# Channel-wise denominators in a linear attention, and four pieces of its surroundings in another order

## The reference

```python
x = x + hyena_conv(layernorm(x))        # short conv, long conv by DFT, gating
x = x + ffn(layernorm(x))               # first mixture of experts
x = x + linear_attention(layernorm(x))
x = x + ffn(layernorm(x))               # second mixture, the same weights
```

```python
q, k = elu(q) + 1, elu(k) + 1
S = S + k[..., :, None] * v[..., None, :]      # running state
z = z + k                                      # running sum of keys
num = einsum('bhi,bhij->bhj', q, S)
den = sum(q * z, axis=-1, keepdims=True)       # one number per token and head
y = num / (den + 1e-6);  return y @ w_proj
```

## Time and profile before

| | us |
|---|---|
| median of 3 runs | 563.15 |
| lowest and highest | 560.63, 567.77 |
| the profiled execution | 564.55 |
| its span from first to last instruction | 562.7 |

### The profile page before, as it was taken

The page is one execution under the profiler, slowest core; times in us unless marked ns, Lnnn a source line. Parts: engine busy times, 40 slices in busy tenths (PEclk is TensorE's granted clock), DMA queues, the critical chain, the costliest instruction groups (busy, mean ns, idle before and its releaser), DMA issues.

```text
span 562.7 us, 13019 instructions
## 1 busy us (share of the span) xinstructions
PE 485.5 (86%) x3852; PEld 372.8 (66%) x3852; DVE 360.7 (64%) x1134; ACT 267.0 (47%) x715; POOL 329.0 (58%) x448
## 2 busy tenths in 40 slices
PE   3989999987888888887899999998878869888883
PEld 1668778865656888864566666666655546888861
DVE  6598999667556455445777787678665545545534
ACT  3554444524532444434777668666543513434430
POOL 4454776277460555552998888888476440555540
PEclk9999999989789999999999999999888889999997
DMA  8999900001011222215000000000011111222228
GB/s 285 320 403 405 404 34 0 2 23 48 29 49 33 77 78 77 77 38 151 1 2 2 2 3 2 3 1 2 3 42 48 33 46 30 77 69 77 71 76 257
DMA packets 36993, 47.56 MB, mean 85 GB/s; under 512 B 4186, under 2 KB 28123, under 8 KB 36798
## 3 DMA queue, kind: packets, MB, share of 16 engines
q1 hardware_dynamic: 31648, 35.90, 19.6%
q0 software_dynamic: 4544, 9.35, 4.9%
q10 hardware_dynamic: 734, 1.50, 0.8%
HBM read 17.86 MB, written 28.87 MB: 83 GB/s over the span
## 4 chain that ended last, share of the span: by engine, by line
PE 66%; DVE 9%; ACT 9%; issue 8%; another core or an unknown queue 4%; POOL 1%; DVEq 1%; DMA 0%; ACTq 0%; POOLq 0%
PE bank L778 61%; ACT silu_sh L1232 2%; PE bank L305 2%; DVE prod L1593 1%; ACT row_in_t L1207 1%; PE bank L888 1%; ACT wide L1207 1%; ACT rows L1225 1%; DVE conv_xv L1500 1%; ACT scores_odd L1207 1%; PE bank L1168 1%; PE bank L790 1%; ACT k_tok L1207 1%; DVE residual L1599 1%
## 5 line engine op out<-in xcount | busy, mean ns | idle before, releaser
L658 POOL DMA_INDIRECT routed<-row_out,row_token x78 | 75.1, 963 | 93.8 <-ACT row_out L1207 61.1
L778 PE MATMUL bank<-row_in_t,row_weights 128*128 128x128 f32 x624 | 84.9, 279 | 15.8 <-ACT row_in_t L1207 12.4
L778 PEld LDWEIGHTS bank<-row_in_t,row_weights 128*128 128x128 f32 x624 | 75.7, 191 | 21.8 <-ACT row_in_t L1207 15.6
L649 POOL DMA_INDIRECT sorted_rows<-rows,place x64 | 62.8, 981 | 38.2 <-issue 15.3
L1273 ACT ACTIVATE row_silu<-bank 128x256 f32<-128x256 f32 x78 | 30.2, 387 | 68.7 <-PE bank L778 48.1
L1645 DVE TENSOR_TENSOR row_act<-row_silu,bank 128x256 f32<-128x256 f32 x78 | 32.7, 419 | 40.1 <-ACT row_silu L1273 24.9
L778 PE MATMUL bank<-wide,weights_sb 128*128 128x512 f32 x112 | 56.1, 642 | 0.0
L778 PE MATMUL bank<-weights_sb,prod 128*128 128x128 f32 x256 | 39.7, 306 | 16.1 <-DVE residual L1599 8.2
L1232 ACT ACTIVATE silu_sh<-bank 128x512 f32<-128x512 f32 x32 | 18.9, 595 | 72.6 <-PE bank L778 54.5
L778 PEld LDWEIGHTS bank<-weights_sb,prod 128*128 128x128 f32 x256 | 34.8, 212 | 24.4 <-DVE residual L1599 11.7
L778 PE MATMUL bank<-experts,row_act 128*128 x312 | 49.5, 281 | 1.1 <-ACT row_out L1207 0.6
(11 more groups left out here) (192 smaller groups left out, 1092.8 us busy)
## 6 DMA issues: line engine op xcount, KB each, us to landing
sorted_rows<-zeros SPq DMA_DIRECT2D x1, 17028.0 KB, 50.9
row_in<-sorted_rows SPq DMA_DIRECT2D x78, 64.5 KB
rows<-routed SPq DMA_DIRECT2D x8, 256.0 KB, 4.9
scores_odd<-routed SPq DMA_DIRECT2D x8, 256.0 KB, 4.4
out<-residual SPq DMA_DIRECT2D x8, 256.0 KB, 3.0
routed<-row_out,row_token POOLq DMA_INDIRECT x78
tables_sb<-tables SPq DMA_DIRECT2D x1, 1024.0 KB, 9.0
experts<-rt_gate SPq DMA_DIRECT2D x1, 1024.0 KB, 18.2
```

Of the source, the lines that this page charges most:

```text
L649: pool.indirect_dma_start(sorted_rows, bass.IndirectOffsetOnAxis(ap=place[:, t:t + 1].bitcast(U32), axis=0), rows[:, t, :], None).then_inc ...
L658: pool.indirect_dma_start(routed, bass.IndirectOffsetOnAxis(ap=row_token[:, r:r + 1].bitcast(U32), axis=0), row_out[:, r, :], None).then_i ...
L778: return pe.matmul(out_, lhsT, rhs, start=start, stop=stop, **kw)
```

## The change

Six things change. **One**, the denominators are made in channel layout at once: PE multiplies by `own_head` (128x128, ones where two channels have the same head), which sums over a head and spreads in one matmul of 256 columns into bank 0; ACT adds epsilon while copying it to SBUF (`att_den_copy`); DVE inverts 128x256 numbers in place. The spreading copy, the two transposes and the old copy are gone. **Two**, in DVE's iteration `att_shift` of batch n+5 stands ahead of this inversion, instead of in the next iteration. **Three**, POOL's `pair_rstd` of the second mixture are spread over iterations 3 to 12, rank and place of pair 0 move one iteration forward, and with them its sends, from iteration 14 to 13. **Four**, at the attention's opening the first mixture's last `down` and its `gate_up` move behind the first batches' norm, and DVE makes two of the four masked copies of q of batch 0. **Five**, ACT issues an Exp of one element ahead of the attention. **Six**, at the kernel's end the additions of pairs 2 to 6 stand ahead of `add_shared` of the last pair.

```diff
-        den_wide, recip = spect_y[:, 0, 0:L], spect_y[:, 0, L:2 * L]
-        den = sb("den", [P, AT * HEADS])
+        den = spect_y[:, :, 0:L]
...
             pipelined([(2, att_qz), (3, att_by_head), (2, clear_future(0)), (5, att_rstd), (2, clear_future(1)),
-                       (0, beside({10: rstds(0), 11: rstds(1), 12: rstds(2, 3), 13: rstds(4, 5), 14: first_send,
-                                   15: second_send}, 2))], B, 2)
+                       (0, beside({3: rstds(0), 5: rstds(1), 7: rstds(2), 9: rstds(3), 10: rstds(4), 12: rstds(5),
+                                   13: first_send, 14: second_send}, 2))], B, 2)
...
                 pe.wait_ge(a_qz, b + 1)
-                wait(pe, a_y, b)
-                for t in range(AT):
-                    last = mm(pe, bank[2][:, 2 * P + t * HEADS:2 * P + (t + 1) * HEADS], qz[:, r, t * P:(t + 1) * P],
-                              head_of)
-                last.then_inc(a_den_mm, 1)
+                pe.wait_ge(a_v, min(b + 2, B))
+                wait(pe, a_den_copied, b)
+                if b == B - 1:
+                    pe.wait_ge(e_route, routed_to("is_top", 1, 0))
+                mm(pe, bank[0][:, L:2 * L], own_head, qz[:, r, :]).then_inc(a_den_mm, 1)
...
-            pipelined([(2, att_scores(0)), (0, att_out), (1, att_recip), (4, att_turn), (1, att_values), (2, att_scores(1)),
-                       (2, att_turn_keys), (0, beside({12: gates_at(0), 13: gates_at(1), 14: opening, 15: closing}, 2)),
-                       (4, att_project), (2, att_state), (2, att_den),
-                       (0, beside({11: turns(0), 12: turns(1), 13: turns(2)}, 2))], B, 2)
+            pipelined([(2, att_scores(0)), (0, att_out), (4, att_turn), (2, att_den), (1, att_values), (2, att_scores(1)),
+                       (2, att_turn_keys), (0, beside({12: gates_at(0), 13: second_gate, 14: opening, 15: closing}, 2)),
+                       (4, att_project), (2, att_state),
+                       (0, beside({11: turns(0), 12: turns(1), 13: turns(2)}, 2))], B, 2, beside_batches)
...
+            act.activation(held[:, 14:15], held[:, 15:16], ACT.Exp)
...
+                act.activation(den[:, r, :], bank[0][:, L:2 * L], ACT.Identity, bias=held[:, 12:13]
+                               ).then_inc(a_den_copied, 1)
...
-                gate_up(LATER + 1, 0)
...
+            def att_first_by_head(i, r):
+                if (i, r) == (0, 0):
+                    dve.wait_ge(a_qk, 1)
+                    for j in FIRST_BY_VECTOR:
+                        dve.tensor_scalar(q_by_head[:, 0, j, :], qk(0)[:, 0:L], head_in_group[:, j:j + 1], 1.0,
+                                          ALU.mult, ALU.mult).then_inc(a_first_by_head, 1)
...
-                dve.tensor_scalar(den[:], bank[2][:, 2 * P:2 * P + AT * HEADS], ATT_EPS, None, ALU.add
-                                  ).then_inc(a_den, 1)
-                dve.wait_ge(a_den, 2 * b + 1)
-                dve.reciprocal(den[:], den[:]).then_inc(a_den, 1)
+                dve.wait_ge(a_den_copied, b + 1)
+                dve.reciprocal(den[:, r, :], den[:, r, :]).then_inc(a_den, 1)
...
-            pipelined([(1, att_den), (1, att_state), (4, att_shift), (3, att_feature_sum), (2, att_mask(0)), (0, att_add),
+            pipelined([(1, att_state), (3, att_feature_sum), (3, att_first_by_head), (2, att_mask(0)), (0, att_add),
                        (5, att_in), (0, att_stats), (3, att_k_sum), (0, beside({14: third_apply}, 2)), (1, att_divide),
-                       (2, att_mask(1)), (0, beside({11: first_apply, 12: first_choice, 13: second_choice,
+                       (2, att_mask(1)), (5, att_shift), (2, att_den), (0, beside({11: first_apply, 12: first_choice, 13: second_choice,
                                                      14: third_choice, 15: third_place}, 2))],
-                      B, 2, {-4: later_gate_up, -3: later_add})
+                      B, 2, {-4: later_gate_up, -3: second_gate_up, -2: later_add})
...
             add_routed(dve, 1, 0, PAIR)
+            gate_up(LATER + 1, 0)
+            add_routed(dve, 1, PAIR, PAIR)
             gate_up(LATER + 1, 1)
-            add_routed(dve, 1, PAIR, PAIR)
+            for k in range(2, LATER + 1):
+                add_routed(dve, 1, k * PAIR, PAIR)
             add_shared(LATER + 1)
-            for k in range(2, PAIRS):
-                add_routed(dve, 1, k * PAIR, PAIR)
+            add_routed(dve, 1, (LATER + 1) * PAIR, PAIR)
```

More of the change, by code:

```diff
@@ L49 @@
 WE = 2 * I + IB * D
-CONSTS = 8
+CONSTS = 9
 RT = TILES + E - 1
@@ L671, in _ @@
             pool.memset(held[:, 13:14], 0.5).then_inc(const_made, 1)
+            pool.memset(held[:, 12:13], ATT_EPS).then_inc(const_made, 1)
             pool.wait_ge(const_made, CONSTS - 2)
@@ L736, in att_by_head @@
                 wait(pool, a_score, AT * GROUPS * (b - 1))
-                for j in range(IN_GROUP):
+                if b == 1:
+                    pool.wait_ge(e_down, PAIRS)
+                heads = range(IN_GROUP) if b else FIRST_BY_POOL
+                for j in heads:
                     pool.tensor_scalar(q_by_head[:, r, j, :], qk(b)[:, 0:L], head_in_group[:, j:j + 1], 1.0,
-                                       ALU.mult, ALU.mult).then_inc(a_by_head, 1)
+                                       ALU.mult, ALU.mult).then_inc(a_by_head, IN_GROUP // len(heads))
             def clear_future(t):
@@ L810, in rank @@
                 pe.wait_ge(e_route, routed_to("chosen_b", m, k))
+                if k == 0 and m == 1:
+                    pe.wait_ge(a_masked, N_MASKED * B)
                 if K:
@@ L922, in row_tiles, with last_down @@
                 up(LATER + 1)
+            def last_down():
                 down(LATER + 1)
-            return turn, gate, rank, up_half, pairs, row_tiles
+            return turn, gate, rank, up_half, pairs, row_tiles, last_down
         @block.tensor
@@ L1032, in tables_there @@
                 pe.wait_ge(tables_loaded, 16)
-            turn, gate, rank, up_half, pairs, row_tiles = experts_pe(pe, 0)
+            turn, gate, rank, up_half, pairs, row_tiles, last_down = experts_pe(pe, 0)
             def first_turn():
@@ L1158, in att_values @@
                 last.then_inc(a_values, 1)
-            def att_recip(i, r):
-                b = 2 * i + r
-                pe.wait_ge(a_wide, b + 1)
-                pe.wait_ge(a_v, min(b + 3, B))
-                if b >= B - 2:
-                    pe.wait_ge(e_route, routed_to("is_top", 1, b - (B - 2)))
-                for t in range(AT):
-                    last = pe.transpose(bank[0][:, (2 + t) * P:(3 + t) * P], den_wide[:, t * P:(t + 1) * P], ident)
-                last.then_inc(a_recip, 1)
             def att_out(i, r):
@@ L1177, in att_out @@
                 last.then_inc(a_out, 1)
-            turn, gate, rank, up_half, pairs, row_tiles = experts_pe(pe, 1)
+            beside_batches = {-3: last_down}
+            turn, gate, rank, up_half, pairs, row_tiles, last_down = experts_pe(pe, 1)
             def turns(k):
@@ L1922, in second_choice @@
             def second_choice():
+                find_place(0)
                 choose(1)
@@ L1929, in third_choice @@
             def third_choice():
-                find_place(0)
+                find_place(1)
                 gate_up(0, 0)
                 choose(2)
-                find_place(1)
             def third_place():
```

52 lines of the change are left out of this document (27 added, 25 removed).

## The result

| | before | changed |
|---|---|---|
| median, us (20 runs each) | 563.49 | 566.87 |
| lowest, highest | 559.0, 568.14 | 560.17, 571.81 |
| the profiled execution's span | 562.7 | 563.3 |

The ratio of changed to before is 1.009, 95% interval 1.0058 to 1.0122: slower by about 5 us, where 1.4 us less was forecast (a median of 561.7, within 553 to 570). On another chip the changed kernel gave 1.0057 [1.0021, 1.0093], with medians of 566.86 and 564.44.

The account below looks back on a forecast made before the run. PE was taken to set the attention's pace, with POOL 1 us and DVE 2 us behind. -4.7 + 0.8 + 3.3 + 0 + 0.2 - 1.0 = -1.4 us against the median 563.15 gave 561.7 us, range 553 to 570.

Parts of the forecast that it names:

- Step 3: Second-mixture rstds in iterations 3, 5, 7, 9: POOL overflows, delay mostly covered; 0.2 each, +0.8 us, bounds 0 and 2.9.
- the two loops: In the attention, dependencies through mask, shift, inversion and state, or feature sum and POOL's rstd: both stay under 7.83 us.
- step 2: DVE's inversion in the attention loop takes 1.76 us and stays covered; gain 0.39 us for each of 12 batches, -4.7.
- Steps 1 and 2: Attention loop: PE's dropped transposes cut the period from 8.22 to 7.83 us; the inversion at 1.76 us stays covered; -4.7.
- Step 4: Attention's end, iterations 11 to 13: the longer inversion delays normalisations PE waits for; +0.9, +0.4 and +2.0, in all +3.3 us.
- step 5: Scatter one iteration earlier: first scatter some 7 us earlier, but no effect on PE's row tiles; 0 us.
- Step 6: Attention's opening: moved table load, Exp and copies gain nothing; the moved down stands ahead of batch 1's turn; +0.2 us.
- Step 7: Kernel's end: one addition instead of six behind add_shared, output DMAs already full; -1.0 us, between 0 and 3.1 gained.
- Rival A: Attention's middle: the inversion becomes the bound on DVE, from 2.09 us upward; 566.8 us, or 575.9 at 2.82; chance 0.25.

Follow-up runs that it names:

- edge: Changed kernel with second-mixture rstds 0 to 2 in iterations 11 to 13 behind q times key sum, 3 to 5 ahead of the first scatters: 0.9966, repeated 0.9973.
- Experiments 2 to 4: Early rstds alone on the kernel before: 1.0024; changed kernel, early rstds behind q times key sum: 1.0053; changed kernel, denominator matmul behind values: 1.0068, without early rstds 1.0051.
- experiment 10: Earlier scatter undone or isolated in several kernels; the one cited here, rank, place and scatters of pairs 0 and 1 an iteration earlier on the kernel before: 1.0005.
- experiment 5: Changed kernel with the inversion on 32 of the 256 columns, the other 224 left uninverted: 1.0050.
- experiment 11: Changed kernel with the opening as before: 1.0087; the changed kernel once more: 1.0057.
- the kernel of experiment 9: Kernel before with only the denominators in channel layout and the shift ahead of the inversion (parts one and two): 1.0024.
- the first one of experiment 10: Changed kernel with all of part three undone: rstds late, rank, place and scatters of pairs 0 and 1 an iteration later: 1.0031.
- experiment 3: Changed kernel with each early rstd of the second mixture issued by POOL behind q times key sum instead of ahead of it: 1.0053.
- experiment 8: As edge, with DVE's normalisations of pairs 0, 1 and 2 in iterations 11 to 13 ahead of the inversion: 1.0021 against the kernel before.

## Why the prediction was wrong

**Step 3 failed.** "I take 0.2 each, +0.8 us", with the words that most of it is covered because the matmul starts 2 us after the scores. Each of the four costs 1.0, 4.0 us in all, above even the bound of 2.9. A fifth stands ahead of `value_c` in iteration 10, in both kernels (rstd 0 before, rstd 4 now). Step 3 did not count it; with the matmul at the iteration's end it was free. Now it costs 1.0 too: the period from batch 13 to 14 is 11.19, and 10.18 in edge, which has no rstd there. In both PE waits 1.53 us for the turn of that period:

```profile
388.39 0.66 PE L793 MATMUL bank<-tables_sb,normed 128*128 128x128 f32 x4 [1.53 <-DVE normed L1502]
```

That makes 5.0 us. Undoing the early rstds takes the ratio from 1.009 and 1.0057 to 0.9986 and 0.9984, 4 to 6 us, across chips.

The bound was wrong because I priced POOL's overflow of work (0.73) and not the arrival of `value_c`. By arrival it is 0.23 + 1.85 + 0.72 = 2.80 us behind the scores, for a matmul that could start at 1.94. The rows of before would have given about half of that: with this trace's 0.23, 0.23 + 1.33 + 0.88 = 2.44. The rest is that the rstd took 1.85 us here. Experiments 2 to 4 show the mechanism: alone it is free, behind `value_c` it costs 0.58, and with the matmul moved 0.38. In these two the delay goes from POOL's own rstd to shift, inversion and `state`, parts of the two loops that step 2 named and held to stay under the period.

**Steps 1 and 2.** The transposes are gone and the inversion is right within 0.02 us. The period is 7.98, not 7.83. Before, PE's starts were 0.33 us apart from the state matmul (of keys and values) to what follows, and 0.55 from the output projection to what follows (300.67 in the earlier trace rows):

```profile
298.28 0.49 PE L778 MATMUL bank<-v_wide,k_tok 128*128 128x128 f32 x2 [0.29 <-ACT k_tok L1207]
298.61 0.52 PE L778 MATMUL bank<-tables_sb,value_c 128*128 128x16 f32 x4
...
300.12 0.71 PE L778 MATMUL bank<-weights_sb,gated 128*128 128x128 f32 x4
```

In the changed kernel they are 0.41 to the scores and 0.62 to the turn:

```profile
301.30 0.49 PE L781 MATMUL bank<-v_wide,k_tok 128*128 128x128 f32 x2 [0.29 <-ACT k_tok L1214]
301.71 1.14 PE L781 MATMUL bank<-prod,silu_sh 32*128 32x512 f32 x8
302.79 0.71 PE L781 MATMUL bank<-weights_sb,gated 128*128 128x128 f32 x4
303.41 0.41 PE L305 MATMUL bank<-tables_sb,normed 128*128 128x128 f32 x2
```

That is -0.24 and not -0.39 a batch: -2.9 for -4.7. The estimate of 2.22 us from the Trainium skill ("VectorE: DVE Perf Modes", section "First, the fixed hardware budget"), its repeat count of 8 read as cycles a column, does not hold here: from 32 to 256 columns the inversion grows from 0.353 to 1.744 us, 6.2 ns each.

**Step 4.** Predicted +3.3. From the first scores of batch 13 to the last values the changed kernel needs 4.5 us more (2.1, 1.3 and 1.1), of which 1.0 is the rstd's of iteration 10. PE waits 1.53, 1.09 and 3.17 us ahead of the three turns, where it waited 0.23, nothing and 1.44. The earlier scatter, which step 5 put at nothing, can arise in the same stretch; on the kernel before it adds 4.0 up to the last values (experiment 10). The inversion's own share is smaller than I thought: taken away almost whole (experiment 5), it takes 1.8 off the three waits and 0.7 off the last values. The size was near, the reason half right.

**Step 5** said 0 and the time says 0 on the kernel before, by two effects of 4 us that cancel, which I had not seen. **Step 6** said +0.2; it is +2.5 and +1.3 on the spot in the two profiles. The step that it left out is PE's clock behind the idle 3.06 us. The idle time itself costs nothing, as the first turn starts 6.66 us after the last `up` began and did so at 6.62 before; and where the clock stayed at 1.00 the first scores came at 13.4. At the end no gain from undoing it is seen (experiment 11). **Step 7** said -1.0. The output queue is as full (share 1.12 at 557 to 560, 1.01 before) and the last addition is 0.6 later in the profile, 0.1 counted from the last `up`. Steps 6 and 7 together are worth nothing that can be told: the kernel of experiment 9 has neither, the first one of experiment 10 has both, and they gave 1.0024 and 1.0031 on one chip.

With the rstds at 5.0 instead of 0.8, the loop at -2.9 instead of -4.7, and the rest as predicted, the sum is -1.4 + 4.2 + 1.8 = +4.6 us: near the +2.4 to +5 measured. The rest as predicted is not shown, so that this fits is in part luck. Rival A had 566.8, the right number for a wrong reason: the inversion is not the bound, as experiment 5 shows. Its sum also has a slip that changes nothing above: by step 3's own way POOL overflows by 0.53 a time in a period of 8.03, not 0.45, and by nothing in one of 8.56, where 2.9 us were added.

**Open:** how the loss in the loop reaches the end. That it does is shown by the ratios with and without the early rstds, but the attention's marks do not order the times: edge ends its attention 7 us behind the kernel before and is not slower, while the first kernel of experiment 10 ends it 3 us behind and gave 1.0031. How much of what the attention loses the second mixture takes back differs from execution to execution (61.0 us from last values to row tiles in one profile of the changed kernel, 58.2 in the other). Open as well: why the opening's gain never reaches the end, and the earlier scatter beside the new denominators.

## What to carry to other kernels

When a matmul moves forward in an engine's order, ask for the arrival time of each of its inputs on the engine that makes them, with everything that is queued ahead there, and not whether that engine has room in the period. Two moves that are each free (a small operation placed into slack, a consumer pulled forward) can cost together, so price them as a pair. And a wait that is taken away on an in-order engine must be followed to whatever stands next behind the instruction that was moved.

## What the hardware showed that I had not expected

- The same `pow` on 128x4 takes POOL 1.01 us in the kernel before and 1.53 in the changed one at the place above, and 1.01 again in experiment 3, where it stands behind `value_c`; what runs beside it was not varied for this.
- The same idle time of PE can be followed by different clocks. In the opening 3.06 us are followed by a projection at 2.07 us in one profile and at 1.13 in two others, and the `down` behind it takes 3.24, 3.40 and 1.95 us; the first scores then come 16.0, 14.7 and 13.4 us after the last `up`. In experiment 8 the values of the last batch take 4.54 us for 1.95, behind a wait of 2.90. The granted clock there is 0.68 of 2.4 GHz as a mean over 32 us, so a part ran at 1.2 GHz.
- The inversion on DVE costs 6.2 ns a column (353 ns for 32, 1744 for 256); a straight line through both leaves 0.155 us fixed.
